# A mixture of 32 experts whose down product is taken from three rounded records, with the down matrix standing still

## The chip, the cores and the metric

One core of a Trainium2 chip runs the whole program. The metric is the device time of one execution in microseconds (us). The kernel before takes 2516.23 us, the median of three runs (2514.08 to 2517.62). Engines are named as in the profile: PE is TensorE, DVE VectorE, ACT ScalarE, POOL GpSimd; SP issues most transfers.

## The reference

Two layers over x (128 sequences of 32 tokens, 128 features), each with cross attention, self attention and a mixture of experts, every one behind a LayerNorm and added to x. The change touches the last part, layer 1's mixture of 32 experts of 64 hidden units, 8 chosen for a token, and a shared expert of the same size:

```python
def body(acc, expert):
    wg, wu, wd, w = expert
    h = jax.nn.silu(flat @ wg.T) * (flat @ wu.T)
    return (acc + w[:, None] * (h @ wd.T), None)
out, _ = jax.lax.scan(body, jnp.zeros_like(flat), (expert_gate, expert_up, expert_down, combine.T))
shared = jax.nn.silu(flat @ shared_gate_w.T) * (flat @ shared_up_w.T) @ shared_down_w.T
out = out + shared
```

All 32 experts are computed for every token; the weight w is zero for those not chosen.

## The kernel before

The program is a chain of stages, each a block that ends in a barrier. The last two are `stage_alibi` (self attention of layer 1; its last four steps also prepare the mixture's weights) and `stage_moe1`, the mixture.

**Tiles.** The 4096 tokens are 32 tiles of 128, in 8 groups g of 4 tiles (512 tokens). The 33 experts are taken two at a time in 17 chunks c of 128 hidden units (the shared expert alone is the last, 64). A **unit** v is one chunk for one group: 136 units, group after group.

**A unit** goes through four engines:

1. PE, `up`: six matmuls of 512 columns into two PSUM banks, gate and up. Each product is made of three matmuls of rounded (fp32r) records, high times high, high times low, low times high, in the helper `product` (L109, L110, L111).
2. ACT, `silu` (L2704): silu of the gate bank into `sg`.
3. DVE, `up` (L2800): `hh` = up bank times `sg`, 128x512.
4. POOL, `weigh` (L2848): `hh` times `cb`, the tokens' weights for the chunk's two experts, in place.
5. PE, `down` (L2642): four matmuls in fp32, each with 128 tokens of `hh` standing and the chunk of `wd` moving, summed over the 17 chunks of the group in PSUM bank 6 or 7, tokens by features.

There are two pairs of banks for gate and up, two `sg`, three `hh`. PE's order is written out: `up(v)`, then `down(v - LAG)` with LAG = 2. Every engine takes its work in the order of the code, so that a wait holds all that stands behind it.

**Beside the units**, DVE computes the routing of the next group in ten parts (`rank`, one behind each of the units c = 0 to 9: L2743 to L2791), the low record of the next group's tokens (`low`, L2735, at c = 12), and adds a group's sum to x (`out`, L2806, at c = 2 of the next group). PE turns the weights of the next group (`turn_combined`, L2621, at c = 10), ACT copies them out (L2697), SP writes them to DRAM and reads them back, spread over the partitions, as `cb`. DVE's `rank` and `low` read SBUF alone; its `up` and `out` read one operand from PSUM.

**Weights.** `moe1_weights` gives the raw matrices and `wide`, the records of the gate and up matrices. The last four steps of `stage_alibi` fill a quarter of `wide` each: ACT rounds (L2448), POOL subtracts (L2527). Outside the engines named, `keep_clock` (L1727) issues PE matmuls without use in idle stretches.

## Time and profile before

| | us |
|---|---|
| median of 3 runs | 2516.23 (2514.08 to 2517.62) |
| the profiled execution | 2514.22 |
| its span, first to last instruction | 2511.3 |
| PE busy | 2369.4 (94%) |
| DVE, ACT, POOL busy | 1694.4 (67%), 1435.8 (57%), 1029.3 (41%) |
| mean granted clock | 0.967 |
| `stage_moe1`'s units, first L109 to the last result | 2187.0 to 2508.6 |
| of these 2189 to 2508.5: PE, DVE, ACT, POOL busy | 316.6, 156.1, 85.5, 179.4 of 319.5 |

The page gives shares over the whole program, a dozen stages with different limits; what a unit costs is read from the time line of one unit, and what an engine's instruction waits for from the rows of two engines side by side. An instruction's time in the trace includes time in which it has been started and can't go on, so that two instructions of one form can show different times.

### The profile page before, as it was taken

Reading aid. Unit: us, or ns where it says so; the run is one execution under the profiler, and the core shown is the slowest. Engines: PE = TensorE matmul, PEld = TensorE weight load, DVE = VectorE, ACT = ScalarE, POOL = GpSimd, SP = SyncE. Lnnn points to the kernel's source line nnn. Section 1 sums busy time; section 2 is a strip of 40 time slices with the busy share of each in tenths; the row PEclk is TensorE's granted clock in tenths of the full one; section 3 lists DMA queues with packets and bytes.
Section 4 is the critical chain, followed back from the end, with each engine's and each line's share of the span. In section 5 each row is a group of like instructions: output and inputs, shape, how many; then the busy total and the mean of one; then the engine's idle time right before and its main releaser. Section 6 shows DMA issues by size and latency. Waiting matters only on the chain. (4 is left out here: it accounts for less than half of the span.)

```text
span 2511.3 us, 93358 instructions
## 1 busy us (share of the span) xinstructions
PE 2369.4 (94%) x38650; PEld 1994.0 (79%) x38650; DVE 1694.4 (67%) x3230; ACT 1435.8 (57%) x3966; POOL 1029.3 (41%) x1068
## 2 busy tenths in 40 slices
PE   7999999999988999998789998999999899899999
PEld 5999999999877888886567666777777678888888
DVE  4777777777686777765967766777777667545453
ACT  4666666666576666674654446777777644422222
POOL 2444444444340000001734435666666533355555
PEclk9999999999999999998979998999999989799999
DMA  6554444444262111110046312100010100166563
GB/s 215 206 183 165 151 153 164 159 151 151 78 246 75 42 43 49 42 42 2 1 101 112 74 35 63 31 25 25 25 31 25 45 18 0 33 121 136 108 123 79
DMA packets 69010, 221.62 MB, mean 88 GB/s; under 512 B 7231, under 2 KB 21059, under 8 KB 60043
## 3 DMA queue, kind: packets, MB, share of 16 engines
q1 hardware_dynamic: 68878, 219.77, 30.0%
q8 instruction: 93, 1.52, 0.3%
q14 instruction: 39, 0.32, 0.1%
HBM read 198.11 MB, written 21.64 MB: 88 GB/s over the span
## 5 line engine op out<-in xcount | busy, mean ns | idle before, releaser
L579 POOL TENSOR_TENSOR l_pn<-l_probs,l_rden 128x1024 f32<-128x1024 f32 x128 | 242.2, 1893 | 404.4 <-DVE l_rden L415 404.4
L512 ACT ACTIVATE l_probs<-ps,l_nmax 128x257 f32<-128x257 f32 x512 | 235.9, 474 | 243.3 <-DVE l_nmax L409 228.3
L981 POOL TENSOR_TENSOR l_probs<-l_probs,l_rden 128x1024 f32<-128x1024 f32 x128 | 242.3, 1893 | 170.8 <-DVE l_rden L832 170.8
L917 ACT ACTIVATE l_probs<-ps,l_nmax 128x257 f32<-128x257 f32 x512 | 235.9, 474 | 59.9 <-DVE l_nmax L826 59.9
L409 DVE TENSOR_REDUCE l_nmax<-ps 128x2 f32<-128x514 f32 x256 | 164.9, 685 | 123.2 <-PE ps L291 123.2
L2848 POOL TENSOR_TENSOR m_hh<-m_hh,m_cb 128x512 f32<-128x512 f32 (+1 forms) x136 | 179.4, 1320 | 141.9 <-DVE m_hh L2800 134.6
L291 PE MATMUL ps<-l_ctxQ,l_q 32*128 32x257 f32 x3072 | 204.1, 394 | 9.3 <-ACT l_q L519 9.0
L2800 DVE TENSOR_TENSOR m_hh<-ps,m_sg 128x512 f32<-128x512 f32 (+1 forms) x136 | 93.9, 691 | 168.7 <-PE ps L111 152.8
L2704 ACT ACTIVATE m_sg<-ps 128x512 f32<-128x512 f32 (+1 forms) x136 | 81.3, 598 | 220.0 <-PE ps L111 219.1
L826 DVE TENSOR_REDUCE l_nmax<-ps 128x2 f32<-128x514 f32 x256 | 165.3, 687 | 61.1 <-PE ps L718 57.9
L837 DVE COPY l_pT<-ps 128x512 f32<-128x512 f32 x256 | 164.8, 686 | 52.2 <-PE ps L727 48.0
L291 PEld LDWEIGHTS ps<-l_ctxQ,l_q 32*128 32x128 f32 x3072 | 146.7, 185 | 34.7 <-issue 16.9
L1436 POOL CAST enc_xt<-enc_xs 128x256 fp32r (+1 forms) x32 | 12.8, 402 | 363.2 <-PE ps L111 363.2
L419 DVE STREAM_TRANSPOSE l_pT<-l_pn 128x1024 f32<-128x1024 f32 x128 | 157.5, 1230 | 0.0
L2642 PEld LDWEIGHTS ps<-m_wd,m_hh 128*128 128x128 f32 (+1 forms) x1088 | 141.4, 191 | 16.9 <-issue 5.7
L2642 PE MATMUL ps<-m_wd,m_hh 128*128 128x128 f32 (+1 forms) x1088 | 144.0, 275 | 2.3 <-POOL m_hh L2848 2.3
L727 PE MATMUL ps<-ident,l_probs 128*128 128x128 f32 x1024 | 133.2, 273 | 0.8 <-DVE x L846 0.4
L304 PEld LDWEIGHTS ps<-l_pT,l_ctxK 32*96 32x96 f32 x4096 | 122.2, 160 | 3.2
L304 PE MATMUL ps<-l_pT,l_ctxK 32*96 32x128 f32 x4096 | 124.6, 269 | 0.0
L304 PE MATMUL ps<-l_pT,l_early 32*96 32x128 f32 x4096 | 123.6, 268 | 1.0 <-DVE x L429 1.0
L304 PEld LDWEIGHTS ps<-l_pT,l_early 32*96 32x96 f32 x4096 | 120.8, 158 | 4.3 <-issue 1.4
L242 PE MATMUL ps<-l_xnT,l_A 128*128 128x128 f32 x768 | 122.0, 298 | 2.1 <-DVE l_xnT L399 0.8
(381 smaller groups left out, 6278.2 us busy)
## 6 DMA issues: line engine op xcount, KB each, us to landing
l_ctxQ<-in_ctx_q SPq DMA_DIRECT2D x32, 1542.0 KB, 6.6
m_cb<-combined SPq DMA_DIRECT2D x64, 512.0 KB, 10.4
l_ctxK<-in_ctx_k SPq DMA_DIRECT2D x16, 1536.0 KB, 6.5
l_early<-in_ctx_k SPq DMA_DIRECT2D x16, 1536.0 KB, 6.4
enc_dash<-kept SPq DMA_DIRECT2D x32, 512.0 KB, 3.3
l_ctxT<-in_ctx_t SPq DMA_DIRECT2D x32, 385.5 KB, 3.4
m_cb<-combined SPq DMA_DIRECT2D x16, 768.0 KB, 16.0
kept<-enc_va SPq DMA_DIRECT2D x10, 512.0 KB, 3.4
```

Source lines behind the costliest of these rows:

```text
L291: last_i = nc.tensor.matmul(ps[:, S_B + hg, 0:NK], q1[r:r + N, j, c, b, :], ctxQ[r:r + N, j, c, b * NK:b * NK + NK], start=c == 0, stop=c ...
L304: last_i = nc.tensor.matmul(ps[0:C, W_B + h, 0:P], ctxK[j][r:r + N, b, m, :], pT[r:r + N, b % 2, :, m, :], start=m == 0, stop=m == NB - 1)
L409: nc.vector.tensor_reduce(nmax[:, par, 2 * half:2 * half + 2], ps[:, S_B + 2 * half:S_B + 2 * half + 2, 0:NK], AX.X, ALU.max, negate=True) ...
L419: nc.vector.transpose(pT[:, b % 2, :, :, :].rearrange("p g m n -> p (g m n)"), pn[:, b % 2, :, :].rearrange("p g n -> p (g n)")).then_inc( ...
L512: nc.scalar.activation(probs[:, par % 2, hg, :], ps[:, S_B + hg, 0:NK], ACT.Exp, bias=nmax[:, par, hg:hg + 1], accum_out=den[:, par, hg:hg ...
L579: nc.gpsimd.tensor_tensor(pn[:, b % 2, :, :], probs[:, b % 2, :, 0:NK - 1], rden[:, b, :, None].to_broadcast([P, HG, NK - 1]), ALU.mult).t ...
L826: nc.vector.tensor_reduce(nmax[:, b, 2 * half:2 * half + 2], ps[:, S_B + 2 * half:S_B + 2 * half + 2, 0:NK], AX.X, ALU.max, negate=True).t ...
L837: nc.vector.tensor_copy(pT[:, b % 2, kt, :], ps[:, T_B + kt, :]).then_inc(pt_ok, 1)
L917: nc.scalar.activation(probs[:, b, hg, :], ps[:, S_B + hg, 0:NK], ACT.Exp, bias=nmax[:, b, hg:hg + 1], accum_out=den[:, b, hg:hg + 1]).the ...
L981: nc.gpsimd.tensor_tensor(pr, pr, rden[:, b, :, None].to_broadcast([P, HG, K_W]), ALU.mult).then_inc(norm_ok, 1)
L2642: last = nc.tensor.matmul(ps[:, ACC + g % 2, n * P:n * P + D], hh[0:rows, v % 3, n * P:n * P + P], wd[0:rows, c, :], start=c + n == 0, sto ...
L2848: nc.gpsimd.tensor_tensor(h, h, cb[0:rows, c, :], ALU.mult).then_inc(h_ok, 1)
```

## The change

The down product is taken as the up products are: from three matmuls of rounded records, 512 tokens moving at a time and the chunk of the down matrix standing. For that

- `wds`, two records of the down matrix, are made in the last four steps of `stage_alibi`, a quarter each: ACT rounds, POOL subtracts. The raw matrices are now freed before `stage_moe1`.
- each unit's weighted `hh` is split: ACT rounds all 512 columns (`high`, into `hs[0]`), then DVE subtracts for columns 128 to 511 and POOL for columns 0 to 127 (`rest_of`, into `hs[1]`). Each engine does this for unit v - 1 behind its own work on unit v.
- `down` has three matmuls and runs with LAG = 3.
- the sum is features by tokens, so that each group's has to be turned: ACT copies the bank to `yT` (`out_turned`, 128x512), PE transposes it in four pieces into bank 5 (`turn_out`, at c = 4 of the next group), and DVE adds from there (`out`, now at c = 5).

```diff
--- before.py
+++ after.py
@@ -2275,13 +2275,16 @@
     return bufs, [(b, w[n]) for b, (n, size) in zip(bufs, sizes)]
 
 
-def moe1_weights(nc, ctx, w):
+def moe1_weights(nc, ctx, raw, w):
 
     cols = (E1 + 1) * I1
-    sizes = {"wg": [P, cols], "wu": [P, cols], "wd": [P, E1 // 2 + 1, D], "gate": [P, E1], "lower": [P, 8, 8]}
-    bufs = {n: ctx.enter_context(nc.sbuf_tensor(f"m1_{n}", size, F32)) for n, size in sizes.items()}
-    loads = [(bufs[n], w[n]) for n in sizes]
-    bufs["wide"] = ctx.enter_context(nc.sbuf_tensor("m1_wide", [P, 4, cols], F32R))
+    down = [P, E1 // 2 + 1, D]
+    sizes = {"gate": [P, E1], "lower": [P, 8, 8], "wg": [P, cols], "wu": [P, cols], "wd": down}
+    bufs = {"wide": ctx.enter_context(nc.sbuf_tensor("m1_wide", [P, 4, cols], F32R)),
+            "wds": ctx.enter_context(nc.sbuf_tensor("m1_wds", [P, 2] + down[1:], F32R))}
+    for n, size in sizes.items():
+        bufs[n] = (raw if n[0] == "w" else ctx).enter_context(nc.sbuf_tensor(f"m1_{n}", size, F32))
+    loads = [(bufs[n], w[n]) for n in ("wg", "wu", "wd", "gate", "lower")]
     return bufs, loads
 
 
@@ -2294,7 +2297,8 @@
         wq, wk, wv, wo, bo, alibi, hm4 = bufs
         wide, raw = moe["wide"], (moe["wg"], moe["wu"])
         HALF = wide.shape[-1] // 2
-        next_in, wh_ok = sem("next_in"), sem("wh_ok")
+        wds, wd = moe["wds"], moe["wd"]
+        next_in, wh_ok, dh_ok = sem("next_in"), sem("wh_ok"), sem("dh_ok")
         DA = DH1 + 1
         wqs = sb("wqs", [P, D])
         shift = sb("shift", [P, T])
@@ -2337,6 +2341,10 @@
+        def down_part(n):
+            n_units = wds.shape[2]
+            return slice(n * n_units // 4, (n + 1) * n_units // 4)
...
@@ -2446,6 +2454,8 @@
                     if t == T - 4:
                         act.wait_ge(next_in, 16 * len(next_loads))
                     nc.scalar.copy(wide[:, 2 * m, cols], raw[m][:, cols]).then_inc(wh_ok, 1)
+                    few = down_part(t + 4 - T)
+                    nc.scalar.copy(wds[:, 0, few, :], wd[:, few, :]).then_inc(dh_ok, 1)
 
             act.sem_inc(v_ok, 1)
             rstd_act(nc, k, act, ln)
@@ -2526,6 +2536,9 @@
                     pool.wait_ge(wh_ok, t + 5 - T)
                     nc.gpsimd.tensor_tensor(wide[:, 2 * m + 1, cols], raw[m][:, cols], wide[:, 2 * m, cols].bitcast(F32),
                                             ALU.subtract)
+                    few = down_part(t + 4 - T)
+                    pool.wait_ge(dh_ok, t + 5 - T)
+                    nc.gpsimd.tensor_tensor(wds[:, 1, few, :], wd[:, few, :], wds[:, 0, few, :].bitcast(F32), ALU.subtract)
 
             run(pool, step)
 
@@ -2533,14 +2546,15 @@
 def stage_moe1(nc, k, bufs, out_dram, comb_d):
 
     NX, NG, NCH, RANK_OPS = E1 + 1, T // 4, E1 // 2 + 1, 14
-    NV, TURN_AT, LAG = NG * NCH, 10, 2
+    NV, TURN_AT, LAG, OUT_AT = NG * NCH, 10, 3, 4
+    SHARE = 128
     BLOCKS = [(0, 2), (2, 6), (6, 12), (12, NCH)]
     with ExitStack() as ctx:
         sb = lambda n, s: ctx.enter_context(nc.sbuf_tensor(f"m1_{n}", s, F32))
         sbr = lambda n, s: ctx.enter_context(nc.sbuf_tensor(f"m1_{n}", s, F32R))
         sem = lambda n: k.sem(f"m1_{n}")
         ps = k.ps
-        wd, wide, gate, lower = [bufs[n] for n in ("wd", "wide", "gate", "lower")]
+        wds, wide, gate, lower = [bufs[n] for n in ("wds", "wide", "gate", "lower")]
         xs = sbr("xs", [P, T, 2, P])
         xn4, xf = sb("xn4", [P, 2, 4, D]), sb("xf", [P, T, P])
         shift = sb("shift", [P, T])
@@ -2551,12 +2565,16 @@
         gt, eq = sb("gt", [P, 4, 8, 8]), sb("eq", [P, 4, 8, 8])
         comb, ct, cb = sb("comb", [P, T, NX]), sb("ct", [NX, 512]), sb("cb", [P, NCH, 512])
         sg, hh = sb("sg", [P, 2, 512]), sb("hh", [P, 3, 512])
+        hs = [sbr(f"hs{m}", [P, 2, 512]) for m in range(2)]
+        yT = xf[:, 0:4, :].rearrange("p t n -> p (t n)")
         (ln, sh_ok, xv_ok, xa_ok, xt_mm, xf_ok, xh_ok, xl_ok, lg_mm, sg_sc, ones_ok, rk) = [sem(n) for n in (
             "ln sh_ok xv_ok xa_ok xt_mm xf_ok xh_ok xl_ok lg_mm sg_sc ones_ok rk").split()]
         (g_mm, u_mm, sg_ok, hh_ok, h_ok, dn_mm, cb_ok, ct_mm, ct_ok, ct_out, x_ok, stored) = [sem(n) for n in (
             "g_mm u_mm sg_ok hh_ok h_ok dn_mm cb_ok ct_mm ct_ok ct_out x_ok stored").split()]
+        (hi_ok, lo_ok, ls_ok, yo_ok, yt_mm) = [sem(n) for n in (
+            "hi_ok lo_ok ls_ok yo_ok yt_mm").split()]
         back = [sem(f"back{n}") for n in range(len(BLOCKS))]
-        GU_B, CT_B, ACC = 0, 4, 6
+        GU_B, CT_B, Y_B, ACC = 0, 4, 5, 6
         X_B, L_B, FIRST_B = 0, 2, 5
         turned_in = lambda g: xf[:, 4 * g:4 * g + 4, :]
         group = lambda m, g: xs[:, 4 * g:4 * g + 4, m, :]
@@ -2634,14 +2652,26 @@
 
             def down(v, g, c):
                 rows = rows_of(c)
-                pe.wait_ge(h_ok, v + 1)
+                pe.wait_ge(lo_ok, v + 1)
+                pe.wait_ge(ls_ok, v + 1)
                 if c == 0 and g > 1:
-                    pe.wait_ge(x_ok, g - 1)
+                    pe.wait_ge(yo_ok, g - 1)
+                pe.nop(nofuse=True)
+                hi, lo = [hs[m][0:rows, v % 2, :] for m in range(2)]
+                wd_h, wd_l = [wds[0:rows, m, c, :] for m in range(2)]
+                to = ps[:, ACC + g % 2, :]
+                nc.tensor.matmul(to, wd_h, hi, start=c == 0, stop=False)
+                nc.tensor.matmul(to, wd_l, hi, start=False, stop=False)
+                nc.tensor.matmul(to, wd_h, lo, start=False, stop=c == NCH - 1).then_inc(dn_mm, 1)
+
+            def turn_out(g):
+                pe.wait_ge(yo_ok, g + 1)
+                if g:
+                    pe.wait_ge(x_ok, g)
                 pe.nop(nofuse=True)
                 for n in range(4):
-                    last = nc.tensor.matmul(ps[:, ACC + g % 2, n * P:n * P + D], hh[0:rows, v % 3, n * P:n * P + P],
-                                            wd[0:rows, c, :], start=c + n == 0, stop=c == NCH - 1 and n == 3)
-                last.then_inc(dn_mm, 1)
+                    last = nc.tensor.transpose(ps[:, Y_B, n * P:n * P + P], yT[:, n * P:n * P + P], k.ident[:, :])
+                last.then_inc(yt_mm, 1)
 
             keep_clock(nc, k, ACC + 1, 8)
             for g in range(NG):
@@ -2667,8 +2697,11 @@
                     down(*units[v - LAG])
                 if c == TURN_AT and g < NG - 1:
                     turn_combined(g + 1)
+                if c == OUT_AT and g:
+                    turn_out(g - 1)
             for v, g, c in units[NV - LAG:]:
                 down(v, g, c)
+            turn_out(NG - 1)
 
         @block.scalar
         def _(act):
@@ -2702,6 +2735,19 @@
                 if v > 1:
                     act.wait_ge(hh_ok, v - 1)
                 nc.scalar.activation(sg[0:rows, v % 2, :], ps[0:rows, GU_B + 2 * (v % 2), :], ACT.Silu).then_inc(sg_ok, 1)
+
+            def high(v, g, c):
+                rows = rows_of(c)
+                act.wait_ge(h_ok, v + 1)
+                if v > 1:
+                    act.wait_ge(dn_mm, v - 1)
+                nc.scalar.copy(hs[0][0:rows, v % 2, :], hh[0:rows, v % 3, :]).then_inc(hi_ok, 1)
+
+            def out_turned(g):
+                act.wait_ge(dn_mm, NCH * g + NCH)
+                if g:
+                    act.wait_ge(yt_mm, g)
+                nc.scalar.copy(yT[:, :], ps[:, ACC + g % 2, :]).then_inc(yo_ok, 1)
 
             rstd_act(nc, k, act, ln)
             act.wait_ge(sh_ok, 1)
@@ -2718,8 +2764,14 @@
             sigmoids(L_B + 1, 16, 32)
             for v, g, c in units:
                 silu(v, g, c)
+                if v:
+                    high(*units[v - 1])
+                if c == LAG and g:
+                    out_turned(g - 1)
                 if c == TURN_AT and g < NG - 1:
                     combined_out(g + 1)
+            high(*units[NV - 1])
+            out_turned(NG - 1)
 
         @block.vector
         def _(dve):
@@ -2796,14 +2848,22 @@
                 dve.wait_ge(sg_ok, v + 1)
                 dve.wait_ge(u_mm, v + 1)
                 if v > 2:
-                    dve.wait_ge(dn_mm, v - 2)
+                    dve.wait_ge(lo_ok, v - 2)
+                if v > 2:
+                    dve.wait_ge(ls_ok, v - 2)
                 nc.vector.tensor_tensor(hh[0:rows, v % 3, :], ps[0:rows, GU_B + 2 * (v % 2) + 1, :], sg[0:rows, v % 2, :],
                                         ALU.mult).then_inc(hh_ok, 1)
 
+            def rest_of(v, g, c):
+                rows = rows_of(c)
+                hi, lo = [hs[m][0:rows, v % 2, SHARE:512] for m in range(2)]
+                dve.wait_ge(hi_ok, v + 1)
+                nc.vector.tensor_tensor(lo, hh[0:rows, v % 3, SHARE:512], hi.bitcast(F32), ALU.subtract).then_inc(lo_ok, 1)
+
             def out(g):
-                dve.wait_ge(dn_mm, NCH * g + NCH)
+                dve.wait_ge(yt_mm, g + 1)
                 xg = k.x[:, 4 * g:4 * g + 4, :]
-                nc.vector.tensor_tensor(xg, ps[:, ACC + g % 2, :].rearrange("p (t d) -> p t d", t=4), xg,
+                nc.vector.tensor_tensor(xg, ps[:, Y_B, :].rearrange("p (t d) -> p t d", t=4), xg,
                                         ALU.add).then_inc(x_ok, 1)
 
             nc.vector.memset(comb[:, :, E1:NX], 1.0).then_inc(ones_ok, 1)
@@ -2824,12 +2884,15 @@
             dve.wait_ge(sg_sc, 3)
             for v, g, c in units:
                 up(v, g, c)
-                if c == LAG and g:
+                if v:
+                    rest_of(*units[v - 1])
+                if c == OUT_AT + 1 and g:
                     out(g - 1)
                 if c < 10 and g < NG - 1:
                     rank(g + 1, c)
                 if c == 12 and 0 < g < NG - 1:
                     low(g + 1)
+            rest_of(*units[NV - 1])
             out(NG - 1)
 
         @block.gpsimd
@@ -2847,10 +2910,19 @@
                 h = hh[0:rows, v % 3, :]
                 nc.gpsimd.tensor_tensor(h, h, cb[0:rows, c, :], ALU.mult).then_inc(h_ok, 1)
 
+            def rest_of(v, g, c):
+                rows = rows_of(c)
+                hi, lo = [hs[m][0:rows, v % 2, 0:SHARE] for m in range(2)]
+                pool.wait_ge(hi_ok, v + 1)
+                nc.gpsimd.tensor_tensor(lo, hh[0:rows, v % 3, 0:SHARE], hi.bitcast(F32), ALU.subtract).then_inc(ls_ok, 1)
+
             for g in range(NG):
                 high(g)
             for v, g, c in units:
                 weigh(v, g, c)
+                if v:
+                    rest_of(*units[v - 1])
+            rest_of(*units[NV - 1])
 
 
 def program(nc, d, out, scratch, kept, combined):
@@ -2868,8 +2940,9 @@
             stage_moe0(nc, k, {n[2:]: a for n, a in d.items() if n.startswith("m_")}, heads_loads, combined)
             al, al_loads = alibi_weights(nc, layer1, {n[2:]: a for n, a in d.items() if n.startswith("s_")})
             stage_heads(nc, k, {n[3:]: a for n, a in d.items() if n.startswith("a1_")}, heads, d["ctx_t"], scratch, al_loads)
-            moe, moe_loads = moe1_weights(nc, layer1, {n[2:]: a for n, a in d.items() if n.startswith("g_")})
-            stage_alibi(nc, k, al, moe, moe_loads)
+            with ExitStack() as raw:
+                moe, moe_loads = moe1_weights(nc, layer1, raw, {n[2:]: a for n, a in d.items() if n.startswith("g_")})
+                stage_alibi(nc, k, al, moe, moe_loads)
             stage_moe1(nc, k, moe, out, combined)
```

Two places show the order on an engine before and now.

DVE, in the units c = 1 to 3 of a group, before (`m_hh` is the unit's product, `m_gt`, `m_eq` and `m_gs` belong to the routing):

```order
L2800 TENSOR_TENSOR m_hh<-ps,m_sg 128x512
L2748 TENSOR_TENSOR m_gt<-m_gs 128x256
L2749 TENSOR_TENSOR m_eq<-m_gs 128x256
L2800 TENSOR_TENSOR m_hh<-ps,m_sg 128x512
L2806 TENSOR_TENSOR x<-ps,x 128x512
L2752 TENSOR_TENSOR m_eq<-m_eq,m_lower 128x256
L2800 TENSOR_TENSOR m_hh<-ps,m_sg 128x512
L2756 TENSOR_TENSOR m_gt<-m_gt,m_eq 128x256
```

and now:

```order
L2854 TENSOR_TENSOR m_hh<-ps,m_sg 128x512
L2861 TENSOR_TENSOR m_hs<-m_hh,m_hs 128x384
L2800 TENSOR_TENSOR m_gt<-m_gs 128x256
L2801 TENSOR_TENSOR m_eq<-m_gs 128x256
L2854 TENSOR_TENSOR m_hh<-ps,m_sg 128x512
L2861 TENSOR_TENSOR m_hs<-m_hh,m_hs 128x384
L2804 TENSOR_TENSOR m_eq<-m_eq,m_lower 128x256
L2854 TENSOR_TENSOR m_hh<-ps,m_sg 128x512
L2861 TENSOR_TENSOR m_hs<-m_hh,m_hs 128x384
L2808 TENSOR_TENSOR m_gt<-m_gt,m_eq 128x256
```

A subtraction of the unit before stands between every `up` and the routing's part, and the addition to x has gone to c = 5.

PE, around the end of a unit, before:

```order
L109 MATMUL ps<-m_xs,m_wide 128x512
L110 MATMUL ps<-m_xs,m_wide 128x512
L111 MATMUL ps<-m_xs,m_wide 128x512
L2642 MATMUL ps<-m_wd,m_hh 128x128 x4
L109 MATMUL ps<-m_xs,m_wide 128x512
```

and now, at c = 4, where a finished group is turned:

```order
L111 MATMUL ps<-m_xs,m_wide 128x512
L2663 MATMUL ps<-m_hs,m_wds 128x512
L2664 MATMUL ps<-m_hs,m_wds 128x512
L2665 MATMUL ps<-m_hs,m_wds 128x512
L2673 MATMUL ps<-ident,m_xf 128x128 x4
L109 MATMUL ps<-m_xs,m_wide 128x512
```

Four matmuls of 128 columns have become three of 512, and once a group four transposes follow.

## Rows read from the trace of the kernel before

**Rows 1.** Windows; a stretch of the mixture; us, then each engine's busy time, clock, DMA:

```profile
2270.00:2310.00 40.00, 40.00 (x247) 34.83 (x246) 21.09 (x46) 10.75 (x18) 22.74 (x18) 1.00 0.55 118
```

**Rows 2.** Time line of PE, one unit; start us, duration us, then the instruction:

```profile
2302.80 0.48 PE L109 MATMUL ps<-m_xs,m_wide 128*128 128x512 f32 x1
...
2304.27 1.05 PE L2642 MATMUL ps<-m_wd,m_hh 128*128 128x128 f32 x8
2305.08 0.48 PE L109 MATMUL ps<-m_xs,m_wide 128*64 128x512 f32 x1
```

**Rows 3.** Time line, DVE's addition in two groups that follow each other:

```profile
2235.38 0.68 DVE L2806 TENSOR_TENSOR x<-ps,x 128x512 f32<-128x512 f32 x1
2275.01 0.68 DVE L2806 TENSOR_TENSOR x<-ps,x 128x512 f32<-128x512 f32 x1
```

**Rows 4.** Time line of PE in layer 0's mixture: rounded matmuls, a transpose, rounded again:

```profile
1400.05 0.39 PE L110 MATMUL ps<-m_xg,m_wide 128*128 128x512 f32 x1
...
1402.61 1.88 PE L1917 MATMUL ps<-m_hh,m_w 128*128 128x512 f32 x4
1404.32 1.05 PE L1930 MATMUL ps<-ident,m_acc 128*128 128x128 f32 x8
1405.13 0.48 PE L109 MATMUL ps<-m_xg,m_sw_wide 128*128 128x512 f32 x1
```

**Rows 5.** Time line of DVE, a unit c = 1:

```profile
2271.73 0.69 DVE L2800 TENSOR_TENSOR m_hh<-ps,m_sg 128x512 f32<-128x512 f32 x1 [1.41 <-PE ps L111]
2272.34 0.42 DVE L2748 TENSOR_TENSOR m_gt<-m_gs 128x256 f32<-128x256 f32 x1
2272.67 1.51 DVE L2749 TENSOR_TENSOR m_eq<-m_gs 128x256 f32<-128x256 f32 x1
```

**Rows 6.** Time line of POOL, the same unit:

```profile
2272.50 1.40 POOL L2848 TENSOR_TENSOR m_hh<-m_hh,m_cb 128x512 f32<-128x512 f32 x1 [0.99 <-DVE m_hh L2800]
```

**Rows 7.** All of L2749: ns min/median/max, first and last start us, shapes:

```profile
L2749 DVE TENSOR_TENSOR m_eq<-m_gs x8: 418/1514/1514, 2171.3 to 2431.2; 128x256 f32<-128x256 f32 x8
```

**Rows 8.** Time line of DVE and POOL at a group's c = 12:

```profile
2298.29 0.68 DVE L2735 TENSOR_TENSOR m_xs<-m_xf,m_xs 128x512 fp32r<-128x512 f32 x1
...
2298.45 1.66 POOL L2848 TENSOR_TENSOR m_hh<-m_hh,m_cb 128x512 f32<-128x512 f32 x1 [0.99 <-DVE m_hh L2800]
```

**Rows 9.** POOL: three weighings back to back; 128 columns; all weighings (ns min/median/max):

```profile
2197.29 3.78 POOL L2848 TENSOR_TENSOR m_hh<-m_hh,m_cb 128x512 f32<-128x512 f32 x3 [3.61 <-DMA m_cb<-combined]
...
L2523 POOL TENSOR_TENSOR x<-x,al_bo x32: 452/455/459, 2008.1 to 2147.0; 128x128 f32 x26, 128x128 f32<-128x128 f32 x6
...
L2848 POOL TENSOR_TENSOR m_hh<-m_hh,m_cb x136: 1260/1297/1663, 2190.8 to 2505.3; 128x512 f32<-128x512 f32 x128, 64x512 f32<-64x512 f32 x8
```

**Rows 10.** ACT by line: silu from PSUM, rounding in SBUF (ns min/median/max):

```profile
L2704 ACT ACTIVATE m_sg<-ps x136: 590/599/600, 2189.1 to 2503.8; 128x512 f32<-128x512 f32 x128, 64x512 f32<-64x512 f32 x8
...
L2448 ACT CAST m_wide<-m_wg x2: 1055/1055/1055, 2140.1 to 2146.9; 128x1056 fp32r<-128x1056 f32 x2
```

**Rows 11.** Time line of DVE, the routing's parts at c = 4 and 9:

```profile
2279.58 0.41 DVE L2759 TENSOR_REDUCE m_gm<-m_gt 128x32 f32<-128x256 f32 x1
2280.02 1.05 DVE L2761 TENSOR_SCALAR m_gm<-m_gm 128x32 f32<-128x32 f32 x1
...
2291.41 1.20 DVE L2791 TENSOR_TENSOR m_comb<-m_rest,m_tot 128x128 f32<-128x128 f32 x1
```

**Rows 12.** Time line, the end of the mixture:

```profile
2505.30 1.26 POOL L2848 TENSOR_TENSOR m_hh<-m_hh,m_cb 64x512 f32<-64x512 f32 x1 [0.98 <-DVE m_hh L2800]
...
2506.71 1.13 PE L2642 MATMUL ps<-m_wd,m_hh 64*128 64x128 f32 x8 [0.48 <-POOL m_hh L2848]
2507.87 0.69 DVE L2806 TENSOR_TENSOR x<-ps,x 128x512 f32<-128x512 f32 x1 [2.65 <-PE ps L2642]
```

**Rows 13.** Time line, the end of the stage before the mixture:

```profile
2157.57 2.41 POOL L2527 TENSOR_TENSOR m_wide<-m_wu,m_wide 128x1056 fp32r<-128x1056 f32 x1 [0.46 <-ACT m_wide L2448]
...
2162.85 1.28 ACT L91 ACT_TABLE_LOAD   x1 [2.04 <-PEq L2290]
```

## Prediction

> **What bounds the kernel now.** The windows come first: in a stretch inside the mixture PE is busy all 40.00 us at a granted clock of 1.00, DVE 21.09, POOL 22.74, ACT 10.75 [rows 1]. So PE sets the pace here, and each unit's down product is on its path. PE's time line gives a unit: `up` from 2302.80 to 2304.27, 1.47 us, `down` to 2305.08, 0.81 us, 2.28 in all [rows 2]. A group of 17 units takes 2275.01 - 2235.38 = 39.63 us [rows 3]; 17 x 2.28 = 38.8, and the rest is the turning of the weights.
>
> The time lines of DVE and POOL side by side tell what the averages hide. L2749 takes 0.418 us where POOL rests, ahead of the units, and 1.514 in the median [rows 7]. In a group it starts at 2272.67, ends at 2274.18, and POOL's weighing ends at 2273.90 [rows 5, 6]: DVE stood until POOL was nearly through (2274.18 - 0.42 = 2273.76, 0.14 before POOL's end) and then ran its 0.42. It holds the other way too: `low` (L2735) starts at 2298.29 and the weighing at 2298.45 takes 1.66 us [rows 8], 0.36 more than the median of 1.30 [rows 9]; the one of rows 6 takes 1.40 and has waited 0.10 for L2748. So a DVE instruction with both inputs in SBUF and a POOL one exclude each other: I take it that POOL has the port for 1.30 - 0.14 = 1.16 us of a weighing, DVE for about a column's time each: 0.52 for 512 (2298.29 to 2298.45 + 0.36), 0.26 for 256 (2272.34 to 2272.60). DVE's `up` reads PSUM and is not seen to wait. Today this costs nothing, since DVE is idle half the time.
>
> **What PE gains.** In layer 0's mixture eleven rounded matmuls of 512 columns take 1402.61 - 1400.05 = 2.56 us, 0.233 each [rows 4]. A unit would have nine: 2.09 instead of 2.28, since the slower first matmul behind an fp32 one goes too. 0.19 x 136 = 26 us less. `turn_out` adds per group four transposes, 0.81 (1404.32 to 1405.13) and 0.09 for the switch back [rows 4]: 0.90. If PE still set the pace a group would take 17 x 2.09 + 0.90 + 0.7 (weights turned) = 37.1, 2.5 less than now.
>
> **What DVE, POOL and ACT get.** Per unit:
> - ACT rounds 512 columns. 1056 take 1.055 us in SBUF, silu's 512 take 0.60 [rows 10]: 0.60. ACT then has 1.2 of 2.1 us.
> - DVE subtracts 384 columns, both inputs in SBUF: 0.40 of the port, 0.47 of the engine (512 columns: 0.68 long, `up`'s successor starts 0.61 behind it [rows 5, 8]).
> - POOL subtracts 128 columns: 0.455 by L2523; from 1056 in 2.41 and 512 in 1.30, 2.05 ns a column, one gets 0.51 [rows 9, 13]. I take 0.45 of the engine, 0.33 of the port. Weighings back to back are (3.78 - 1.30) / 2 = 1.24 apart [rows 9].
>
> By sums this fits: port 0.40 + 1.16 + 0.33 = 1.89 of 2.09. In order it does not, because each subtraction waits for ACT, ACT for the weighing, and DVE's next `up` stands behind the subtraction. Follow two units from the start of a weighing of v, t = 0: POOL weighs v to 1.24 and subtracts for v - 1 to 1.69, then weighs v + 1, with the port until 2.85, end 2.99. ACT rounds v from 1.40 to 2.00; DVE asks for its subtraction at 2.1, gets the port at 2.85, and starts `up(v+2)` at 3.32, which is done at 4.01. ACT has rounded v + 1 at 3.7, so DVE's subtraction follows `up` at once, at 3.92, and takes the port just ahead of the weighing of v + 2, which begins at 4.32. Two units in 4.3: **2.15 a unit**, where PE could do 2.09. LAG = 3 doesn't help: PE has slack, but POOL and DVE are a closed loop.
>
> What lies behind DVE's subtraction comes on top:
> - Routing that needs the port waits out the weighing, and the next weighing needs the next `up`. Engine times: L2748, L2749, L2752, L2756 0.33 each (2272.34 to 2272.67), L2761 0.13 (it too waited: 1.05 for 32 columns), L2764, L2781 and part 9's three (each waits for the one before) 0.20 each as an estimate between 0.13 and 0.33, `low` 0.60 [rows 5, 8, 11]. Sum 1.32 + 0.13 + 1.0 + 0.6 = 3.1 us a group.
> - Five pieces of routing without the port (L2743, L2759, the maxima, `match_replace`, L2784) and `out` come to 6 x 0.44 = 2.6 us, by L2759 (2279.58 to 2280.02 [rows 11]). It hides under the weighing where the subtraction went first, and not where the subtraction waited: half, 1.3.
> - ACT's `out_turned` and L2697, 0.5 each, hold silu and rounding: 1.0.
>
> A group: 17 x 2.15 + 3.1 + 1.3 + 1.0 = 41.9, against 39.63: +2.3, seven times: +16. The last group has no routing: 36.5 + 0.8 = 37.3 against 38.8: -1.5.
>
> The tail is longer. From POOL's end, 2506.56, DVE adds at 2507.87, 1.31 later [rows 12]. Now: ACT 0.7, subtraction 0.6, three matmuls 1.05 (0.7, 0.35 to start), ACT's copy 0.65, transposes 1.13 as L2642's eight passes, hand-overs 0.13: 4.3. +3.
>
> Making `wds` costs nothing: POOL's last part ends at 2159.98, the stage at 2162.85 [rows 13]. Even if POOL's last two new subtractions (1.3, and 1.6 for 640 columns) came fully behind that, they would end at 2162.9; what hides them is the last steps' work on the other engines, and without that cover they cost under 3 us. ACT's roundings, 0.6 each, lie under POOL's.
>
> **Sum**: 16 - 1.5 + 3 = +17.5. The profiled execution took 2514.2, 2.0 under the median: 2531.7 by it, **2534** beside the median. Both ends: POOL's piece at 0.51 instead of 0.45 adds 0.06 x 17 x 8 = 8; if ACT's waits and the half of the hidden routing cost nothing, 2.3 x 7 = 16 goes and it is +1.
>
> The Trainium skill (SBUF — State Buffer, "SBUF: two separate sides") speaks against this change: a DVE instruction with two SBUF inputs and a GpSimd one take the shared port pair exclusively, whoever starts first, and for the whole instruction. The rows show the exclusion, but a release 0.14 us before POOL's end. With the whole instruction held, every wait for a weighing would last 0.14 longer, some 8 pairs and 8 routing steps a group: 0.14 x 16 x 8 = 18 us more, +35. I go by the rows.
>
> **Rivals.**
> 1. *PE keeps the pace.* The port's demand by sums (1.89 a unit and some 2 us of routing a group, 34 us) is under PE's 37.1, and LAG = 3 with three `hh` could smooth what comes late. Group -2.5 x 7, last -2.4, tail +3: -17, 2499. For it: the sums. Against it: `up(v)` of DVE needs ACT's and PE's work of the same unit only, but stands behind a wait for the port; smoothing needs DVE to be ahead, and it can't be. It decides when DVE's subtraction never waits for a weighing, that is when ACT's rounding is done before `up` ends. This is the case on the other side, not slower.
> 2. *Every subtraction goes first.* The loop locks to the other phase: 0.40 + 1.24 + 0.45 = 2.09 to 2.10 a unit, only routing that needs the port shows: 17 x 2.10 + 3.1 + 0.5 = 39.3, group -0.3, tail +3: 0 to +2, 2517. For it: requests at 2.1 and 1.69 differ by little. Against: a rounding that starts when the weighing ends (plus 0.7) is late by 0.4 for POOL's next start.
> 3. *The change doesn't give rounded speed.* If nine matmuls cost 0.25 each, PE is at 2.25, and the loop hides nothing more: same forecast, since DVE and POOL lead. It would move rival 1 to 2520.
>
> **Chances.** The forecast 0.68, rival 2 0.12, rival 1 0.20. Slower by over 0.2% (5 us, about what a measurement of this kernel can tell): 0.70; within: 0.11; faster: 0.19. The range: the sum's lower end with rival 2 lies at 2517; it reaches to 2503, into rival 1's neighbourhood, and up to 2556, where the whole-instruction wait and a POOL piece of 0.51 lead together in part (+8 and half of 18 over the forecast).
>
> **What would show it.** Right: PE idle before L109 or the new `down` some 0.1 to 0.3 us a unit, waiting for DVE's `hh`; DVE's subtraction alternating between 0.55 and about 1.3 us; weighings alternating between 1.30 and 1.5; a group of 41 to 43 us; L2749 still waiting for POOL. Wrong: PE busy all of a window and groups near 37, or subtractions that all take 0.55. The tail and `wds` are right if the last `up` to the last addition grows by 3 us and the mixture starts when it did.

## The result, and the profile after

The changed kernel takes 2534.12 us (median of 4 runs, 2532.43 to 2538.76), the kernel before 2515.15 in the same series: 1.0087 of it, 95% interval 1.0067 to 1.0106. The profiled execution shown here took 2538.76, the longest of the four. One of e6's ten runs took 5593.57 us and is left out of its ratio.

In the two profiles, whose spans differ by 25.6 us, +22.1 lies in the mixture: its first L109 starts at 2190.5 and its last addition to x at 2533.47, 343.0 us; before it was 2187.0 to 2507.87, 320.9. (The remaining +3.5 lies ahead of it, in stages that are the same in both but for the making of `wds`, on which see below; over the profiles of this case the mixture starts anywhere from 2176.6 to 2201.1, so the groups' lengths are the steadier measure.)

PE is no longer busy throughout. The windows of a stretch inside the mixture, in the columns of [rows 1]:

```profile
2300.00:2340.00 40.00, 36.91 (x154) 26.83 (x154) 32.31 (x52) 19.46 (x34) 33.42 (x33) 1.00 0.60 117
```

PE has 3.1 us of idle time in 40 where it had none; DVE went from 21.1 to 32.3, POOL from 22.7 to 33.4. In this stretch the clock is granted in full, but not in every one. The next shows 0.96, and in the rows of PE behind the turning of the weights (L2639) the rounded matmuls are 0.43 us apart instead of 0.23, the lower of the clock's two levels (1.2 and 2.4 GHz), for some 3 us:

```profile
2320.00:2360.00 40.00, 36.91 (x148) 26.89 (x147) 31.98 (x58) 18.68 (x33) 31.18 (x31) 0.96 0.60 106
...
2346.80 1.00 PE L2639 MATMUL ps<-ident,m_comb 128*33 128x128 f32 x4 [1.65 <-DVE m_comb L2843]
...
2348.02 0.63 PE L110 MATMUL ps<-m_xs,m_wide 128*128 128x512 f32 x1
2348.45 0.63 PE L111 MATMUL ps<-m_xs,m_wide 128*128 128x512 f32 x1
```

PE stood 1.65 us before it fell. It stands as long in the same place of the group before (1.66 at 2304.84), where the clock stays at 1.00, so that no rule follows from it. With the fall the unit c = 10 takes 3.88 us from `up` to `up` instead of 2.31, and its group 43.5 instead of 42.0; the same comes again at 2432, two groups on.

The time line of DVE, in units c = 13 to 15 of a group (no routing) and c = 2 to 4 of the next; L2854 is `up`, L2861 the subtraction, L2804 and L2808 routing (columns: start us, duration us, instruction, idle time before and who ended it):

```profile
2312.60 0.68 DVE L2854 TENSOR_TENSOR m_hh<-ps,m_sg 128x512 f32<-128x512 f32 x1
2313.20 0.54 DVE L2861 TENSOR_TENSOR m_hs<-m_hh,m_hs 128x384 fp32r<-128x384 f32 x1
2313.67 0.68 DVE L2854 TENSOR_TENSOR m_hh<-ps,m_sg 128x512 f32<-128x512 f32 x1
2315.58 1.39 DVE L2861 TENSOR_TENSOR m_hs<-m_hh,m_hs 128x384 fp32r<-128x384 f32 x1 [1.23 <-ACT m_hs L2744]
2316.89 0.68 DVE L2854 TENSOR_TENSOR m_hh<-ps,m_sg 128x512 f32<-128x512 f32 x1
...
2327.06 0.54 DVE L2861 TENSOR_TENSOR m_hs<-m_hh,m_hs 128x384 fp32r<-128x384 f32 x1
2327.52 1.51 DVE L2804 TENSOR_TENSOR m_eq<-m_eq,m_lower 128x256 f32<-128x256 f32 x1
2328.96 0.68 DVE L2854 TENSOR_TENSOR m_hh<-ps,m_sg 128x512 f32<-128x512 f32 x1
2329.56 0.54 DVE L2861 TENSOR_TENSOR m_hs<-m_hh,m_hs 128x384 fp32r<-128x384 f32 x1
2330.02 1.50 DVE L2808 TENSOR_TENSOR m_gt<-m_gt,m_eq 128x256 f32<-128x256 f32 x1
2331.45 0.68 DVE L2854 TENSOR_TENSOR m_hh<-ps,m_sg 128x512 f32<-128x512 f32 x1
```

The pair of units that the prediction followed is there: one subtraction of 0.54, the next waits 1.23 for ACT's rounding and then takes 1.39, and from `up` at 2312.60 to the second next at 2316.89 are 4.29 us. Behind a subtraction that went first, a routing part with two SBUF inputs takes 1.5 us instead of 0.42, and that unit takes 2.49 (2328.96 to 2331.45).

POOL's time line in the same places:

```profile
2315.26 1.28 POOL L2911 TENSOR_TENSOR m_hh<-m_hh,m_cb 128x512 f32<-128x512 f32 x1
2316.50 0.79 POOL L2917 TENSOR_TENSOR m_hs<-m_hh,m_hs 128x128 fp32r<-128x128 f32 x1
2317.64 1.54 POOL L2911 TENSOR_TENSOR m_hh<-m_hh,m_cb 128x512 f32<-128x512 f32 x1 [0.35 <-DVE m_hh L2854]
...
2329.72 1.53 POOL L2911 TENSOR_TENSOR m_hh<-m_hh,m_cb 128x512 f32<-128x512 f32 x1 [0.36 <-DVE m_hh L2854]
```

The weighing at 2315.26 takes its 1.28 and makes DVE wait (the subtraction of 2315.58 ends at 2316.97); then POOL's short subtraction waits for DVE's (0.79 instead of 0.45), and the weighing at 2317.64 waits for the subtraction that went first (1.54 instead of 1.30). The chain of waits inside the units (who waited for whom, us in total, times, longest):

```profile
ACT m_hs L2744 <- POOL m_hh L2911: 130.8, 107, 3.6
POOL m_hh L2911 <- DVE m_hh L2854: 66.4, 90, 5.6
DVE m_hs L2861 <- ACT m_hs L2744: 55.1, 58, 2.1
PEld ps L2663 <- issue: 34.7, 61, 1.9
ACT m_hs L2744 <- PE ps L2665: 22.6, 24, 1.9
...
PE ps L2639 <- DVE m_comb L2843: 11.5, 7, 1.7
...
PE ps L2663 <- issue: 10.3, 22, 1.5
```

The loop of the first three rows, POOL to ACT to DVE and back to POOL, stands where before ACT and DVE waited for PE, and POOL for DVE. PE itself now waits in two places: in front of `down` (L2663, 10.3 us), and, 1.6 us in each of seven groups, in front of the turning of the next group's weights (L2639, 11.5 us), for the last part of DVE's routing (L2843). By lines, PE's last `down` matmul and POOL's subtraction (ns min/median/max, first and last start):

```profile
L2665 PE MATMUL ps<-m_hs,m_wds x136: 385/396/552, 2198.3 to 2531.6; 128*128 128x512 f32 x128, 64*128 64x512 f32 x8
...
L2917 POOL TENSOR_TENSOR m_hs<-m_hh,m_hs x136: 443/638/823, 2196.9 to 2530.2; 128x128 fp32r<-128x128 f32 x128, 64x128 fp32r<-64x128 f32 x8
```

A matmul record of 0.40 is as in [rows 4]; they are issued 0.23 apart. POOL's short subtraction takes 0.638 in the median and 0.443 at least: most of them wait. The tail:

```profile
2525.42 0.40 PE L111 MATMUL ps<-m_xs,m_wide 128*64 128x512 f32 x1
...
2529.49 0.62 ACT L2744 CAST m_hs<-m_hh 64x512 fp32r<-64x512 f32 x1 [1.98 <-POOL m_hh L2911]
...
2532.81 0.63 PE L2673 MATMUL ps<-ident,m_xf 128*128 128x128 f32 x4 [0.77 <-ACT m_xf L2750]
2533.47 0.69 DVE L2866 TENSOR_TENSOR x<-ps,x 128x512 f32<-128x512 f32 x1 [2.78 <-PE ps L2673]
```

From POOL's last weighing's end (2527.95 + 1.51 = 2529.46) to the addition are 4.0 us, 1.3 before [rows 12].

### The profile page after: what moved, and what is told of

Same layout as the page of the kernel before. It is cut to its first block and busy times, and to the rows that moved or that the text cites. A ratio compares the mean times of both kernels' runs of the same rounds, so it can differ in the third digit from the quotient of the medians.

```text
span 2536.9 us, 92774 instructions
## 1 busy us (share of the span) xinstructions
PE 2365.0 (93%) x38002; PEld 1945.8 (77%) x38002; DVE 1804.6 (71%) x3366; ACT 1518.5 (60%) x4114; POOL 1129.9 (45%) x1208
## 5 line engine op out<-in xcount | busy, mean ns | idle before, releaser
L2911 POOL TENSOR_TENSOR m_hh<-m_hh,m_cb 128x512 f32<-128x512 f32 (+1 forms) x136 | 197.3, 1451 | 67.8 <-DVE m_hh L2854 66.8
L2744 ACT CAST m_hs<-m_hh 128x512 fp32r<-128x512 f32 (+1 forms) x136 | 84.4, 620 | 157.6 <-POOL m_hh L2911 134.9
L2861 DVE TENSOR_TENSOR m_hs<-m_hh,m_hs 128x384 fp32r<-128x384 f32 (+1 forms) x136 | 121.9, 896 | 58.6 <-ACT m_hs L2744 58.1
L2248 POOL TENSOR_TENSOR m_acc<-m_acc,m_yb 128x512 f32<-128x512 f32 x56 | 74.7, 1335 | 115.8 <-DVE m_yb L2159 114.8
L727 PEld LDWEIGHTS ps<-ident,l_probs 128*128 128x128 f32 x1024 | 117.1, 142 | 1.9 <-issue 0.7
```

Source lines behind the costliest of these rows:

```text
L727: last_i = nc.tensor.transpose(ps[:, T_B + kt, hg * P:hg * P + P], probs[:, b, hg, kt * P:kt * P + P], k.ident[:, :])
L2911: nc.gpsimd.tensor_tensor(h, h, cb[0:rows, c, :], ALU.mult).then_inc(h_ok, 1)
```

## The experiments

Two measures are used: the ratio to the kernel before with its 95% interval, and the length of a group in the profile, from one addition to x to the next (the starts of L2866 or its like). The mean is from the first to the seventh, divided by six. It mixes three things: groups like each other, groups with a fall of the clock (two in the changed kernel, two in e4, three in e5, one in e3, none in the rest), and, in the changed kernels, a sixth that has only about half of its routing, since the last group has none. The median of the first five leaves the last two out. "Mixture" is from its first L109 to the last addition. "Wait" is PE's, in front of the turned weights, for DVE's last routing part, in seven groups (in e2 for the memset that stands for it).

| kernel | first and seventh addition | mean group | median | mixture | wait | ratio (95%) |
|---|---|---|---|---|---|---|
| before | 2235.38, 2473.18 | 39.63 | 39.63 | 320.9 | none | 1 |
| changed | 2250.97, 2505.07 | 42.35 | 41.98 | 343.0 | 11.5 | 1.0087 (1.0067 to 1.0106) |
| e1, DVE subtracts from PSUM zeros | 2249.46, 2476.44 | 37.83 | 37.80 | 311.8 | 6.2 | 0.9939 (0.9914 to 0.9963) |
| e2, no routing | 2237.31, 2469.72 | 38.73 | 38.73 | 320.6 | 5.5 | 0.9972 (0.9947 to 0.9997) |
| e3, POOL subtracts nothing | 2242.68, 2490.82 | 41.36 | 41.38 | 337.3 | 14.1 | 1.0051 (1.0026 to 1.0076) |
| e4, three record buffers | 2249.57, 2501.78 | 42.03 | 41.70 | 339.7 | 11.5 | 1.0077 (1.0056 to 1.0098) |
| e5, control for e1 | 2260.13, 2514.93 | 42.47 | 41.96 | 345.6 | 11.5 | 1.0088 (1.0055 to 1.0121) |
| e6, DVE subtracts from PSUM copy | 2235.90, 2468.20 | 38.72 | 38.77 | 319.9 | 11.3 | 0.9985 (0.9955 to 1.0015) |
| e7, DVE subtracts a unit later | 2263.67, 2495.09 | 38.57 | 38.90 | 320.5 | 11.0 | 1.0019 (0.9983 to 1.0055) |
| e8, e7 and POOL subtracts nothing | 2257.29, 2489.07 | 38.63 | 38.94 | 319.7 | 12.5 | 0.9995 (0.9977 to 1.0014) |
| e9, e6 and e7 | 2239.29, 2463.77 | 37.41 | 37.48 | 311.6 | 5.0 | 0.9960 (0.9940 to 0.9980) |
| e10, routing ahead of subtraction | 2244.56, 2491.04 | 41.08 | 41.49 | 336.1 | 6.3 | 1.0053 (1.0034 to 1.0073) |

**e1.** The operand, and the bank that it needs free:

```diff
-        GU_B, CT_B, Y_B, ACC = 0, 4, 5, 6
+        GU_B, CT_B, Y_B, FREE_B, ACC = 0, 4, 4, 5, 6
...
-                nc.vector.tensor_tensor(lo, hh[0:rows, v % 3, SHARE:512], hi.bitcast(F32), ALU.subtract).then_inc(lo_ok, 1)
+                nc.vector.tensor_tensor(lo, ps[0:rows, FREE_B, SHARE:512], hi.bitcast(F32), ALU.subtract).then_inc(lo_ok, 1)
```

A memset of the bank ahead of the units, and two waits of PE because banks are shared, are left out of the cut.

> DVE's subtraction takes its first operand from a PSUM bank that holds zeros instead of the unit's product in SBUF; the group's turned sum moves to bank 4 to free bank 5. It leaves out the low record's values of columns 128 to 511, the instruction's size and waits stay. Port theory: with one SBUF operand it waits for no weighing and holds up none, every subtraction takes about 0.55 us, every weighing about 1.30, PE sets the pace again: a group 17 x 2.09 + 1.1 = 36.7 instead of 42.3 us, seven times, the program near 2495 us (0.992 of before). Rival, the chain of waits from POOL over ACT to DVE and back (latency in fixed order, the port does not matter): the chain is unchanged, so a group stays near 42 us and the program near 2534. Rival, POOL's own time is the bound: unchanged too.

The two lines, subtraction and weighing:

```profile
L2864 DVE TENSOR_TENSOR m_hs<-ps,m_hs x136: 540/557/561, 2199.4 to 2500.4; 128x384 fp32r<-128x384 f32 x128, 64x384 fp32r<-64x384 f32 x8
...
L2916 POOL TENSOR_TENSOR m_hh<-m_hh,m_cb x136: 1263/1297/1307, 2197.4 to 2498.5; 128x512 f32<-128x512 f32 x128, 64x512 f32<-64x512 f32 x8
```

In the changed kernel the same two have 536/558/1444 and 1263/1532/1882:

```profile
L2861 DVE TENSOR_TENSOR m_hs<-m_hh,m_hs x136: 536/558/1444, 2196.3 to 2530.1; 128x384 fp32r<-128x384 f32 x128, 64x384 fp32r<-64x384 f32 x8
...
L2911 POOL TENSOR_TENSOR m_hh<-m_hh,m_cb x136: 1263/1532/1882, 2194.3 to 2527.9; 128x512 f32<-128x512 f32 x128, 64x512 f32<-64x512 f32 x8
```

Not one of 136 subtractions waits, the slowest weighing takes 1.307 us, and 4.5 us a group go (4.2 by the medians), with the same instructions and sizes in every unit. Both rivals had said no change. A group is 37.8, not the 36.7 expected. Most of that is PE's wait for DVE's last routing part, 6.2 us in seven groups or 0.9 each; the port itself shows little, in `low` (0.80 us here, 0.68 at least) and POOL's short subtraction behind it:

```profile
2303.28 0.80 DVE L2790 TENSOR_TENSOR m_xs<-m_xf,m_xs 128x512 fp32r<-128x512 f32 x1
...
2303.48 0.92 POOL L2922 TENSOR_TENSOR m_hs<-m_hh,m_hs 128x128 fp32r<-128x128 f32 x1
```

**e5** has only the move of banks, with the same two waits of PE:

```diff
-        GU_B, CT_B, Y_B, ACC = 0, 4, 5, 6
+        GU_B, CT_B, Y_B, FREE_B, ACC = 0, 4, 4, 5, 6
```

> Control for e1: only the move of the turned sum to bank 4, with the two waits that it needs; DVE's subtraction reads SBUF as in the changed kernel. If e1's gain came from the operand, this stays at 1.009 of before (1.006 to 1.011); if from the bank, it falls to 0.994.

1.0088, and a median group of 41.96 us against 41.98: the bank is not what counts in e1.

**e2.** The routing parts leave DVE's loop:

```diff
-                if c < 10 and g < NG - 1:
-                    rank(g + 1, c)
+                if c == 9 and g < NG - 1:
+                    nc.vector.memset(tot[:, 0:1], 1.0).then_inc(cb_ok, 1)
```

> The routing parts of groups 1 to 7 are left out of DVE's loop (one small memset stands for them), so their weights are not computed. Port theory: 3.1 us a group of port users behind the subtraction and 1.3 of the others go: a group 42.3 - 4.4 = 38 us, seven times, near 2503 us. Rival (routing lies in DVE's idle time, as it did before the change): under 10 us gained, 2525 or more.

A group is 3.6 us shorter, 3.3 by the medians. The 3.1 + 1.3 = 4.4 of the sum is not the number to compare: it has `low` (0.6) and `out` (half of 0.44) in it, which e2 keeps, so that 3.6 of it is what e2 takes out. Before the change the same routing lay in DVE's idle time; now most of it is on the path. The remaining 38.73 is the plain loop, 17 x 2.15 = 36.6, and 2.2 for the rest: `low`, `out`, ACT's copies and PE's wait of 0.8 in front of the turned weights, which no run separates. Its time line shows the pair undisturbed:

```profile
2301.85 0.68 DVE L2854 TENSOR_TENSOR m_hh<-ps,m_sg 128x512 f32<-128x512 f32 x1
2302.45 0.54 DVE L2861 TENSOR_TENSOR m_hs<-m_hh,m_hs 64x384 fp32r<-64x384 f32 x1
2302.92 0.67 DVE L2854 TENSOR_TENSOR m_hh<-ps,m_sg 128x512 f32<-128x512 f32 x1
2304.83 1.43 DVE L2861 TENSOR_TENSOR m_hs<-m_hh,m_hs 128x384 fp32r<-128x384 f32 x1 [1.24 <-ACT m_hs L2744]
2306.18 0.68 DVE L2854 TENSOR_TENSOR m_hh<-ps,m_sg 128x512 f32<-128x512 f32 x1
```

**e3.** POOL's part and the waits for it are removed:

```diff
-    SHARE = 128
+    SHARE = 0
...
-                pe.wait_ge(ls_ok, v + 1)
```

> DVE subtracts all 512 columns, POOL none. Port theory with the loop followed: two units take 1.24 (weighing) + 1.16 (port of the next) + 0.60 (subtraction) + 0.61 (up) + 0.53 (next subtraction's port) = 4.14 instead of 4.32, 2.07 a unit, under PE's 2.09; routing on top stays: a group near 41 us, the program near 2524 (2519 to 2534). Rival, POOL's own time is the bound: with only 1.24 us a unit left to POOL, PE sets the pace, near 2497.

41.36 us a group where 41 was expected, and 1.0051. POOL's busy time falls from 33.4 to 25.0 us in a window of 40, and the kernel gains 1.0 us a group, 0.6 by the medians, where the rival had PE's pace: POOL's own time is not the bound. The intervals of the two ratios overlap, so that the gain itself rests on the groups.

```profile
2300.00:2340.00 40.00, 36.83 (x157) 27.31 (x156) 32.77 (x61) 19.85 (x35) 25.04 (x17) 1.00 0.57 116
```

**e4.** `hs` with three buffers:

```diff
-                if v > 1:
-                    act.wait_ge(dn_mm, v - 1)
+                if v > 2:
+                    act.wait_ge(dn_mm, v - 2)
```

The space comes from `xn4`, laid over `hh`.

> Three buffers for the records of the product instead of two, so that ACT's rounding no longer waits for the down product two units back (22.6 us of ACT's waits in the trace). Port theory: that wait lies beside the loop of POOL, ACT and DVE; the program stays at 2534 within 4 us. Rival, buffers bound the loop: the waits go, up to 20 us gained, near 2515.

As the port theory had it: 0.3 us a group, and the intervals of the ratios overlap. The buffers of the records are not the limit; those of `hh`, and LAG, no run changes by themselves.

**e7.** The same work in another order:

```diff
-    NV, TURN_AT, LAG, OUT_AT = NG * NCH, 10, 3, 4
+    NV, TURN_AT, LAG, OUT_AT = NG * NCH, 10, 4, 5
...
-                if v:
-                    rest_of(*units[v - 1])
+                if v > 1:
+                    rest_of(*units[v - 2])
                 if c == OUT_AT + 1 and g:
```

with `hh` of four buffers, `hs` of three, and the waits that go with them.

> DVE subtracts two units behind its up instead of one (POOL still one), with LAG 4, OUT_AT 5, four buffers of the product and three of its records. The record is then always ready, so that the subtraction goes right behind up and ahead of the weighing. The port's demand is the same. Loop theory: 2.10 us a unit, only the routing that needs the port shows: 17 x 2.10 + 3.1 + 0.5 = 39.3 us a group instead of 42.3, near 2513 us, 1.000 of before (0.997 to 1.004). Rival, the port's demand alone counts, not the order: as the changed kernel, 1.009.

A group falls by 3.8 us to 38.57 (by the medians by 3.1, to 38.90), a little more than expected (39.3), with the port's demand as it was. DVE's subtraction waits for ACT's rounding 0.3 us in the whole mixture, where it waited 55.1, and weighings still wait for the port (median 1.540 us). So the time was lost in the order, not in the sum of what the port has to carry. The fourth `hh` buffer and LAG = 4 came with the order here and were not tried alone; e10 below changes the order without them. The whole program's ratio is less clear, 1.0019 with an interval that holds the expected 1.000 and goes to 1.0055; its runs spread from 2503 to 2534. The mixture as a whole is as long as before, 320.5 us to 320.9: the first group, which the measure leaves out, takes 44.1 us from `up` to `up` against 39.8, and eats what the others gain.

**e8.** e7 with e3's edit (`SHARE = 0`).

> As e7, and DVE subtracts all 512 columns. Port 0.53 + 1.16 = 1.69 a unit, so that plain units go at PE's 2.09; routing that needs the port waits out the weighing (some 0.5 us over 2.09 each, seven a group): a group near 39 us, 0.998 of before (0.994 to 1.002). If POOL's short subtraction was what the loop lacked, this is clearly under e7; if DVE's own time is the bound, it is over e7.

38.63: the same as e7 within 0.1. With the order mended, it doesn't matter who subtracts the last quarter. In both, PE waits 11 to 12.5 us in seven groups for DVE's routing.

**e6.** A real version of e1. ACT copies its record to the free bank, one more instruction a unit:

```diff
                 nc.scalar.copy(hs[0][0:rows, v % 2, :], hh[0:rows, v % 3, :]).then_inc(hi_ok, 1)
+                act.wait_ge(hi_ok, v + 1)
+                if v:
+                    act.wait_ge(lo_ok, v)
+                nc.scalar.copy(ps[0:rows, FREE_B, SHARE:512],
+                               hs[0][0:rows, v % 2, SHARE:512].bitcast(F32)).then_inc(hp_ok, 1)
...
-                nc.vector.tensor_tensor(lo, hh[0:rows, v % 3, SHARE:512], hi.bitcast(F32), ALU.subtract).then_inc(lo_ok, 1)
+                nc.vector.tensor_tensor(lo, hh[0:rows, v % 3, SHARE:512], ps[0:rows, FREE_B, SHARE:512], ALU.subtract).then_inc(lo_ok, 1)
```

> Everything is computed. ACT rounds as before and then copies columns 128 to 511 of the high record into the free PSUM bank, and DVE subtracts that, so that it has one SBUF operand. Port theory: the port is free for POOL as in e1, but the subtraction is 0.5 us later each time, and ACT has 1.7 of 2.09 us a unit: a group 38 to 39.5 us, 0.995 to 1.000 of before. Rival (the chain from POOL over ACT to DVE is what costs): the chain is 0.5 us longer in each turn, so it is slower than the changed kernel, over 1.012.

It puts 0.5 us into the very chain that the rival holds responsible, and takes 3.6 us a group away. DVE reads `hh` from SBUF here, as the changed kernel does and e1 doesn't, so that the gain of e1 didn't come from leaving `hh` unread. ACT's busy time goes from 19.5 to 29.8 us in a window of 40, for which DVE's subtraction waits 82.5 us in all, and still the group is shorter:

```profile
2300.00:2340.00 40.00, 38.39 (x168) 29.77 (x167) 29.34 (x63) 29.75 (x56) 30.46 (x36) 1.00 0.63 127
...
L2869 DVE TENSOR_TENSOR m_hs<-m_hh,ps x136: 537/555/556, 2184.8 to 2492.5; 128x384 fp32r<-128x384 f32 x128, 64x384 fp32r<-64x384 f32 x8
...
L2919 POOL TENSOR_TENSOR m_hh<-m_hh,m_cb x136: 1265/1294/1307, 2182.3 to 2490.0; 128x512 f32<-128x512 f32 x128, 64x512 f32<-64x512 f32 x8
```

**e9.** Both: ACT copies the record of unit v - 2 right behind the silu of v, and DVE subtracts it behind `up` of v.

```diff
                 silu(v, g, c)
+                if v > 1:
+                    to_psum(*units[v - 2])
                 if v:
                     high(*units[v - 1])
```

> e6 and e7 together, everything computed: DVE subtracts two units behind, from the PSUM copy that ACT makes right behind the next unit's silu, ahead of its rounding. The port is free for POOL and the copy is ready when up ends. A group as in e1, 37.8 us or a little less (37.4 to 38.2), 0.994 of before (0.991 to 0.997). Rival, ACT's time (1.7 us a unit and two copies a group) is the next bound: a group stays at e6's 38.7 us, 0.998 or more.

37.41 us a group, 0.9960 of the kernel before (0.9940 to 0.9980): it beats the kernel before by 0.4% and the changed one by 1.3%. Of the 1.3 us a group under e6, 0.9 is PE's shorter wait for the routing (5.0 us instead of 11.3 in seven groups). Less this wait, the median groups of e1 and e6 to e9 are all 36.8 to 37.3 us, near the 37.1 of PE's own pace in the prediction. No run shortens the wait by itself. PE is busy 39.57 of 40 us again, against 36.91:

```profile
2300.00:2340.00 40.00, 39.57 (x174) 30.97 (x173) 32.88 (x66) 30.24 (x57) 32.34 (x37) 1.00 0.59 129
```

**e10.** The changed kernel with one move in DVE's loop:

```diff
-                if v:
-                    rest_of(*units[v - 1])
                 if c == OUT_AT + 1 and g:
                     out(g - 1)
...
+                if v:
+                    rest_of(*units[v - 1])
```

> The changed kernel with one thing moved: on DVE the routing part, the addition to x and the low record stand ahead of the subtraction instead of behind it. Loop theory: where the subtraction waits for ACT, the routing without the port now fills the wait (up to 1.3 us a group), while a part that needs the port takes it ahead of the weighing and pushes weighing and subtraction back by its 0.3 instead of waiting 1.2: a group 40 to 41.5 us, 1.003 to 1.007 of before. Rival (the port's demand alone counts): 42.3 us as it is, 1.009.

41.08 and 1.0053, within what was expected, with no work added or taken away. By the medians the order is worth 0.5 us a group (41.49 against 41.98). The rest of the 1.3 is the changed kernel's two falls of the clock, of which this run has none, and the half-routed group (39.03 against 41.19). Whether the order also keeps the clock up, one profile of each can't say. The two intervals still overlap, at 1.0067 to 1.0073.

## Why the prediction was right

The forecast was 2534 us; it is 2534.12. That the last digits agree is luck: the forecast adds 17.5 to 2516.23, the measured difference is 19.0 on 2515.15, and in the profiles the mixture alone grew by 22.1. What was right is the mechanism and the length of a plain group; a term for the clock was missing. Point by point:

- *Which instructions exclude each other*, read from L2749 and L2735 [rows 5 to 8]: right. e1 shows it as a cause: one operand in PSUM instead of SBUF and all waits of the pair are gone.
- *Two units in 4.3 us*: 4.29 in the time line. The phases are as followed, a subtraction that goes first and one that waits for the weighing, 0.54 and 1.39.
- *Routing that needs the port waits out the weighing*: 1.50 and 1.51 us for L2808 and L2804, 2.49 for such a unit (2.16 + 0.33 by the same steps). What e2 takes out was put at 3.6 us a group (4.4 less `low` and `out`); e2 says 3.3 by the medians. The step is not right for every part: L2801, the successor of the L2749 that was named as a sign, takes 0.412 in the median and so mostly doesn't wait, while L2804 and L2808 do (1.510 and 1.502).
- *A group of 41.9*: 41.98 in the median, 42.35 in the mean. Two terms inside it were off and cancel: routing put 0.3 too high, and what is left beside it 0.4 too low, 38.73 in e2 against 37.5 + 0.8 (17 x 2.15 + 1.0, and `low` and `out`). What makes the 0.4 stays open. ACT's rounding takes 0.62, the estimate was 0.60.
- *Seven groups, +16*: +21.0, from the first `up` of the mixture to that of the last group (298.6 us, before 277.6). Seven groups of 41.98 would be +16.3. The falls of the clock in the groups at 2321.2 and 2406.7, for which the sum has no term, add 1.5 each; the first two groups, 42.63 and 43.07 us long, add 1.7.
- *Where PE stands*: 0.19 us a unit, within the 0.1 to 0.3 forecast. But half of it lies in front of the turned weights, waiting for DVE's last routing part; the prediction expected it before `up` and `down`.
- *The last group -1.5 and the tail +3*: together +1.1 instead of +1.5 (from the group's first `up` to the last addition 41.37 us, before 40.26). The tail is +2.7 from the last weighing (4.0 against 1.3). The sign that was named for it, the last `up` matmul to the addition, grew by 4.2 and not by 3: 8.05 us from 2525.42, and before 3.83 (2504.04 to 2507.87), since the last units ahead of the last weighing are late too. The transposes were mis-sized: 0.90 a group was taken from L1930 [rows 4], which I read as transposes. Its four are fp32 matmuls against the identity, two records each; `turn_out` issues `transpose`, one record each, and takes 0.36 to the next L109 (2330.22 to 2330.58), off the path at that:

```profile
2330.22 0.60 PE L2673 MATMUL ps<-ident,m_xf 128*128 128x128 f32 x4
2330.58 0.48 PE L109 MATMUL ps<-m_xs,m_wide 128*128 128x512 f32 x1
```

- *Nothing for `wds`*: no cost can be seen. The last four steps of the stage before take DVE 20.8 us (2144.62 to 2165.40), before 21.9. The sign "the mixture starts when it did" tells nothing, with starts that spread over 24 us. POOL's last piece ended at 2165.39 (2163.85 + 1.54), 1.0 before ACT's first instruction of the mixture at 2166.36, and DVE's last one of the stage before at 2165.80 was later still.
- *PE's gain*: real, and unused in the changed kernel. Nine matmuls follow 0.23 apart (e1 and e9 have PE at 39.2 and 39.6 of 40 us in groups of 37.8 and 37.4).

Of the rivals, "PE keeps the pace" at 0.20 rested on the port's sum, 1.89 of 2.09 us. With the same sum e7's median group is 38.90: the port can carry it, but not in the changed kernel's order. "Every subtraction goes first" is what e7 makes by force, and its group, 38.57 in the mean, is near the 39.3 written for it. The weighing of the Trainium skill's rule (SBUF — State Buffer, "SBUF: two separate sides": the loser waits for the whole instruction) came out as the rows had it: DVE's 1.39 begins at 2315.58, and less 0.54 gives a release at 2316.43, 0.11 before the weighing's end at 2316.54. By the Trainium skill's whole instruction the group would have been estimated 2 us longer, 0.14 x 16, than the sum by rows; the trace agrees with a release ahead of POOL's end.
